# Routed feed-forward stage: results scattered to token order per tile in place of a gather at the end

## What is computed

```python
def _L3_ffn_ref(hidden_states, wg_red, wg, w1, b1, w2, b2):
    x = hidden_states.reshape(-1, c)
    xr = x @ wg_red.T
    wg_unit = wg / jnp.maximum(jnp.linalg.norm(wg, axis=1, keepdims=True), EPS)
    logits = xr @ wg_unit.T
    gates = jax.nn.softmax(logits, axis=1)
    indices_s = jnp.argmax(gates, axis=1)
    scores = jnp.max(gates, axis=1)
    for e in range(E):                      # E = 8 experts, hidden width 512
        mask = (indices_s == e).astype(x.dtype)[:, None]
        h = jax.nn.gelu(x @ w1[e] + b1[e], approximate=False)
        out = out + mask * (h @ w2[e] + b2[e])
    out = out * scores[:, None]
# and around it
g = _silu(_L3_ffn_ref(xn, ...))
x = x + s * g
```

## Time and profile before

| | |
|---|---|
| median of 3 runs | 6424.23 us (6416.99 to 6426.39) |
| profiled execution, its own time | 6420.27 us |
| its span, first to last instruction | 6418.5 us |
| PE busy | 5656.5 us, 88% |
| DVE busy | 4334.3 us, 68% |
| ACT busy | 3828.7 us, 60% |
| POOL busy | 2970.8 us, 46% |
| mean DMA rate | 35 GB/s |

### The profile page before, as it was taken

The page is one execution under the profiler, slowest core; times in us unless marked ns, Lnnn a source line. Parts: engine busy times, 40 slices in busy tenths (PEclk is TensorE's granted clock), DMA queues, the critical chain, the costliest instruction groups (busy, mean ns, idle before and its releaser), DMA issues. The chain is left out here.

```text
span 6418.5 us, 101900 instructions
## 1 busy us (share of the span) xinstructions
PE 5656.5 (88%) x33881; PEld 2996.4 (47%) x33881; DVE 4334.3 (68%) x9917; ACT 3828.7 (60%) x8010; POOL 2970.8 (46%) x2847
## 2 busy tenths in 40 slices
PE   8999998439999799999999889999999999896643
PEld 3444443312222466666666634444444444464443
DVE  4555553246666677777787678888888888685624
ACT  2444444126666577777777667777777777674322
POOL 1225234356777667666666433232332323154355
PEclk9999998769999899999999999999999999999876
DMA  1000001430000111111111110000000000031324
GB/s 38 8 11 30 14 17 34 122 81 11 14 13 8 54 33 32 30 33 39 40 46 44 35 29 12 19 10 12 19 12 19 10 12 17 17 89 44 107 68 122
DMA packets 348505, 225.99 MB, mean 35 GB/s; under 512 B 30290, under 2 KB 324946, under 8 KB 347730
## 3 DMA queue, kind: packets, MB, share of 16 engines
q1 hardware_dynamic: 328624, 183.83, 10.9%
q0 software_dynamic: 12288, 25.19, 1.5%
q10 hardware_dynamic: 7074, 10.46, 0.5%
HBM read 104.24 MB, written 68.55 MB: 27 GB/s over the span
## 5 line engine op out<-in xcount | busy, mean ns | idle before, releaser
L3816 PE MATMUL a_scores_ps<-a_kT,a_q_mixed 128*128 128x512 f32 x2048 | 1046.3, 593 | 3.7 <-ACT a_probs L3626 3.1
L3826 PE MATMUL a_acc_ps<-a_probsT,a_v_post 128*128 128x512 f32 x2048 | 1042.8, 592 | 0.4 <-DVE a_probsT L3719 0.4
L3626 ACT ACTIVATE a_probs<-a_scores_ps,a_neg_max 128x512 f32<-128x512 f32 x1024 | 703.0, 687 | 427.2 <-DVE a_neg_max L3709 417.9
L3709 DVE TENSOR_REDUCE a_neg_max<-a_scores_ps 128x1 f32<-128x512 f32 x1024 | 693.4, 677 | 202.4 <-PE a_scores_ps L3816 197.9
L3719 DVE STREAM_TRANSPOSE a_probsT<-a_probs 128x512 f32<-128x512 f32 x1024 | 715.4, 699 | 135.7 <-PE a_acc_ps L3826 112.2
L3631 ACT ACTIVATE a_probs<-a_probs,a_inv_sum 128x512 f32<-128x512 f32 x1024 | 727.8, 711 | 0.8 <-DVE a_inv_sum L3714 0.8
L2949 DVE TENSOR_REDUCE a_neg_max<-a_pair_ps 128x2 f32<-128x1024 f32 (+3 forms) x512 | 417.6, 824 | 353.8 <-PE a_pair_ps L3045 349.1
L2753 ACT ACTIVATE a_probsT<-a_pair_ps 128x1024 f32<-128x1024 f32 (+3 forms) x512 | 359.4, 704 | 483.8 <-PE a_pair_ps L3058 482.3
L3826 PEld LDWEIGHTS a_acc_ps<-a_probsT,a_v_post 128*128 128x128 f32 x2048 | 389.0, 190 | 490.9 <-issue 488.8
L3816 PEld LDWEIGHTS a_scores_ps<-a_kT,a_q_mixed 128*128 128x128 f32 x2048 | 384.4, 190 | 476.6 <-issue 438.9
L3572 POOL TENSOR_TENSOR a_q_mixed<-a_qT,a_pre 128x512 f32<-128x512 f32 x248 | 250.3, 1041 | 759.8 <-PE a_scores_ps L3816 759.8
(11 more groups left out here) (416 smaller groups left out, 11852.0 us busy)
## 6 DMA issues: line engine op xcount, KB each, us to landing
f_v_even<-f_v_odd SPq DMA_DIRECT2D x224, 130.0 KB, 2.3
attention_out<-a_s_out SPq DMA_DIRECT2D x64, 256.0 KB, 2.3
f_gs<-attention_out SPq DMA_DIRECT2D x64, 256.0 KB, 4.4
a_v<-a_v_rows SPq DMA_DIRECT2D x256, 64.0 KB, 2.1
a_x<-x_after SPq DMA_DIRECT2D x48, 256.0 KB
f_x<-x_after SPq DMA_DIRECT2D x48, 256.0 KB, 5.5
f_gx<-x_after SPq DMA_DIRECT2D x48, 256.0 KB, 3.3
x_after<-f_gout SPq DMA_DIRECT2D x32, 256.0 KB, 2.4
```

Source lines behind the costliest of these rows:

```text
L3626: act.activation(probs[:, n % NPR, :], scores_ps[n % NS][:], ACT.Exp, bias=neg_max[:, n % NS:n % NS + 1], scale=1.0, accum_out=row_sum[:, ...
L3709: dve.tensor_reduce(neg_max[:, n % NS:n % NS + 1], scores_ps[n % NS][:], AX.X, ALU.max, negate=True).then_inc(max_ready, 1)
L3816: pe.matmul(scores_ps[n % NS][:], q_mixed[:, g % 2, i].rearrange("f a q -> f (a q)"), kT[:, par, :], start=True, stop=True).then_inc(score ...
L3826: pe.matmul(acc_ps[par][:], v_post[:, g, i, :], probsT[:, g % NT, i, :], start=(p == 0), stop=(p == U - 1)).then_inc(products_done, 1)
```

## The change

The sorted rows get two more elements. Each row of x is now WIDE = 130 elements wide: 128 features, the number of the token (HOME) and its softmax weight (WEIGHT). The scatter carries both along, so a tile knows where its rows belong and how they are weighted. The rows of `x_sorted` are no longer filled with zeros from SBUF but with a constant array from DRAM, in which every row has a HOME of its own behind the last token, so that unused rows are scattered to a spare area.

In the tile loop, `add_b2` writes to a small buffer `y_tile` of two tiles. ACT multiplies by the weight into `y_tiles` (`weigh`, new), DVE converts the HOME column of each group to integers (`homes_of`, new), and POOL scatters each finished tile to `y_home` in DRAM (`scatter_tile`, new), eight tiles behind `pick_w1`. The gather at the end, DVE's weighting and the store to `y_sorted` are gone. After the last scatter has landed, SP loads the results of a batch from `y_home` with one plain DMA. POOL takes over s * y. The buffers of the finish are four deep where `gx` and `gs` were two deep, and `x_tiles` is six groups deep where it was four.

```diff
-        x = sb("x", [P, batches, NC, D])
+        x = sb("x", [P, batches, NC, WIDE])
-        y_tiles = sb("y_tiles", [P, 2, GROUP, D])
+        y_tile = sb("y_tile", [P, 2, D])
+        y_tiles = sb("y_tiles", [P, 4, GROUP, D])
...
         @block.sync
...
-                sp.dma_start(x_groups[g], zeros[:]).then_inc(zeroed, 16)
+                sp.dma_start(x_groups[g], fill_groups[g]).then_inc(filled, 16)
...
+            for n in range(4):
+                sp.wait_ge(y_scattered[n], 16 * GROUP * len(range(n, GROUPS, 4)))
+            for b in range(min(4, batches)):
+                load_y(b)
             for b in range(batches):
                 sp.wait_ge(out_ready, b + 1)
                 sp.dma_start(out_rows[b], out[:, b % 2]).then_inc(out_stored[b % 2], 16)
-                if b + 2 < batches:
-                    load_gate(b + 2)
+                if b + 4 < batches:
+                    load_y(b + 4)
+                    load_gate(b + 4)
...
         @block.gpsimd
...
+            def scatter_tile(i):
+                g, t = divmod(i, GROUP)
+                if t == 0:
+                    pool.wait_ge(homes_ready, g + 1)
+                pool.wait_ge(y_kept, i + 1)
+                pool.indirect_dma_start(y_home, bass.IndirectOffsetOnAxis(ap=homes[:, i:i + 1], axis=0),
+                                        y_tiles[:, g % 4, t, :], None).then_inc(y_scattered[g % 4], 16)
+            for i in range(TILES + 8):
+                if i < TILES:
+                    pick_w1(i)
+                if i >= 8:
+                    scatter_tile(i - 8)
...
-                    pool.indirect_dma_start(y[:, b % 4, c, :], None, y_sorted,
-                                            bass.IndirectOffsetOnAxis(ap=slot[:, n:n + 1], axis=0)
-                                            ).then_inc(gathered[b % 4], 16)
+                pool.tensor_tensor(gs[:, b % 4], gs[:, b % 4], y[:, b % 4], ALU.mult).then_inc(s_scaled, 1)
         @block.scalar
...
+            def weigh(i):
+                g, t = divmod(i, GROUP)
+                act.wait_ge(y_biased, i + 1)
+                if t == 0 and g >= 4:
+                    act.wait_ge(y_scattered[g % 4], 16 * GROUP * (g // 4))
+                act.activation(y_tiles[:, g % 4, t, :], y_tile[:, i % 2], ACT.Copy,
+                               scale=x_tiles[:, g % 6, t, WEIGHT:WEIGHT + 1]).then_inc(y_kept, 1)
-            for i in range(TILES + 1):
+            for i in range(TILES + 5):
                 if i < TILES:
                     keep_tile(i)
-                if i >= 1:
+                if 0 <= i - 1 < TILES:
                     gelu(i - 1)
+                if 0 <= i - 5:
+                    weigh(i - 5)
         @block.vector
...
+            dve.wait_ge(exp_ready, 1)
+            chain(dve.tensor_reduce(weight[:], diff[:], AX.X, ALU.add))
+            chain(dve.reciprocal(weight[:], weight[:]))
+            dve.tensor_copy(x[:, :, :, WEIGHT], weight[:].rearrange("p (b c) -> p b c", c=NC))
             dve.wait_ge(summed, 1)
...
                 dve.wait_ge(y_done, i + 1)
-                if t == 0 and g >= 2:
-                    dve.wait_ge(y_stored[g % 2], 16 * (g // 2))
-                dve.tensor_tensor(y_tiles[:, g % 2, t, :], y_ps[i % 2][:, 0:D], b2[:, bass.ds(e, D)],
-                                  ALU.add).then_inc(y_kept, 1)
+                if i >= 2:
+                    dve.wait_ge(y_kept, i - 1)
+                dve.tensor_tensor(y_tile[:, i % 2], y_ps[i % 2][:, 0:D], b2[:, bass.ds(e, D)],
+                                  ALU.add).then_inc(y_biased, 1)
+            def homes_of(g):
+                dve.wait_ge(tiles_loaded[g % 6], 16 * (g // 6 + 1))
+                dve.tensor_copy(homes[:, g * GROUP:(g + 1) * GROUP], x_tiles[:, g % 6, :, HOME]).then_inc(homes_ready, 1)
...
             def down(i):
...
-                    pe.wait_ge(y_kept, i - 1)
+                    pe.wait_ge(y_biased, i - 1)
```

More of the change, by code:

```diff
@@ L1437, in sorted_experts_phase @@
                  (rank[:], dram["L3f_rank"]), (below[:], dram["L3f_below"]), (steps[:], dram["L3f_steps"][:, 0:N]),
-                 (tile_no[:], dram["L3f_tile_no"][:, 0:TILES])]
+                 (tile_no[:], dram["L3f_tile_no"][:, 0:TILES]),
+                 (home[:], dram["L3f_home"][:, 0:N])]
         big_loads = [(w1[:], dram["L3f_w1"].rearrange("d n i -> d (n i)")),
@@ L1470, in _ @@
             sp.wait_ge(scattered, 16 * N)
-            for g in range(4):
+            for g in range(6):
                 load_group(g)
[L1473 to L1479, removed]
+            for b in range(min(4, batches)):
+                load_gate(b)
@@ L1480, in _ @@
+            for g in range(6, GROUPS):
+                load_group(g)
+            for n in range(4):
+                sp.wait_ge(y_scattered[n], 16 * GROUP * len(range(n, GROUPS, 4)))
+            for b in range(min(4, batches)):
+                load_y(b)
             for b in range(batches):
@@ L1506, in _, with pick_w1 @@
             pool.wait_ge(slots_ready, 2)
-            for i in range(TILES):
+            def pick_w1(i):
                 e = pool.value_load(at_i[0:1, i:i + 1], min_val=0, max_val=(E - 1) * I)
@@ L1606, in _ @@
             dve.wait_ge(weights, 16 * (len(loads) + 1))
+            dve.tensor_copy(x[:, :, :, HOME], home[:].rearrange("p (b c) -> p b c", c=NC))
             chain(dve.tensor_tensor(wg_sq[:], wg[:], wg[:], ALU.mult))
@@ L1696, in _ @@
                     add_b2(i - 2)
[L1698 to L1706 removed]
+                if i < TILES and i % GROUP == 2:
+                    homes_of(i // GROUP)
+            for b in range(batches):
+                dve.wait_ge(s_scaled, b + 1)
                 dve.wait_ge(sigmoid_ready, b + 1)
[L1708 removed]
+                chain(dve.tensor_tensor(gs[:, b % 4], gs[:, b % 4], gate[:, b % 2], ALU.mult))
                 if b >= 2:
                     dve.wait_ge(out_stored[b % 2], 16 * (b // 2))
[L1711 to L1717 removed]
+                dve.tensor_tensor(out[:, b % 2], gs[:, b % 4], gx[:, b % 4], ALU.add).then_inc(out_ready, 1)
         @block.tensor
@@ L3900, in constants @@
     out["L3f_tile_no"] = np.arange(NB * NC + 8, dtype=np.float32)[None, :]
+    out["L3f_home"] = (128.0 * np.arange(NB * NC)[None, :] + i).astype(np.float32)
+    fill = np.zeros(((NB * NC + 8) * P, D + 2), np.float32)
+    fill[:, D] = NB * T + np.arange((NB * NC + 8) * P)
+    out["L3f_fill"] = fill
     out["L1_window_mask"] = np.where(np.stack([seen & ((w == 1) | (same == 0)), seen], axis=1), 0.0,
```

98 lines of the change are left out of this document (42 added, 56 removed).

## The result

The changed kernel took **6442.4 us** (median of 8 runs, 6439.6 to 6453.7) against 6423.6 for the kernel before (8 runs, 6417.0 to 6426.4): ratio 1.0033, 95% interval 1.0022 to 1.0044. That is 18.8 us slower. Forecast were 6432 us and a range of 6416 to 6458. The profiled execution of after took 6442.71 us, its span 6441.0.

A forecast was written before the change was run, and what follows sets the result against it. Three parts in turn were taken as bound by POOL issuing indirect DMAs, PE, then POOL again. Loop +44.5, loop end +2.9, head +1.0 and last part -40.2 gave +8.2 on 6424.23: 6432 us, range 6416 to 6458.

The forecast's parts named there:

- a circle through `add_b1`, `gelu`, `weigh` and `add_b2`: Tile loop: with two places in `y_tile`, these instructions wait on each other in turn, setting a least 2.56 us a tile.
- The tile loop, forecast +44.5: Tiles 4 to 71: 2.56 us a tile against 1.896, over 67 tiles, 44.5 us added.
- `weigh` itself: a 128x128 ACT instruction took 0.26: Tile loop, on ACT: `weigh` priced at 0.26 us from an instruction that reads PSUM where `weigh` reads SBUF.
- The last part, forecast -40.2: After the tile loop: plain loads of y replace 64 gathers, 56.9 us against 97.1, 40.2 saved.
- the 3.6: End of the last part: 3.6 us from the end of the last DVE instruction to the end of the span.
- The end of the loop and the head: Five scatters behind the last `add_b1` add 2.9 us; the `home` load and earlier weight work before the slots add 1.0.
- The rival: Fill of `x_sorted` from DRAM comes late: at a third of 322 GB/s 3 us beyond cover, at a quarter 6450; chance 0.07.
- PE's pace: Tile loop: waits release earlier than read, so the 44.5 us fall away and the time is 6388; chance 0.13.
- The slower turn by register loads of 0.558: Tile loop: DVE's register load always at its longest, turn 2.82 us, loop 17.4 us longer, 6450; chance 0.13.
- The granted clock: Tile loop: PE's clock falls to the 1.2 GHz level, loop 63 us more, 6495; chance 0.05.
- the first case: Tile loop at 2.4 to 2.65 us a tile, end as forecast: own range 6418 to 6442, chance 0.62.
- three slow cases: Slower tile turns in the loop (0.13), a late fill (0.07) and a fallen PE clock (0.05).

## Why the prediction was right, and where it was off

- *Which way and how.* The forecast (a circle through `add_b1`, `gelu`, `weigh` and `add_b2` eats what the end saves) was right. It is shown from three sides: cutting it in either of two ways gives 1.894 us a tile, making a link shorter by 0.093 makes the period shorter by 0.093, and with the register load ahead the turn is again the sum of its links, 2.06.
- *The tile loop, forecast +44.5, measured +53.4.* This is the step that was off, and in it one term: "`weigh` itself: a 128x128 ACT instruction took 0.26" was 0.385. I had noted that it reads another source, and had left out that it has a scale from SBUF. 67 x 0.125 = 8.4 of the 8.9 us that are missing; three long turns (1.1 us) and a `homes_of` that costs its turn 0.03 and not 0.1 nearly cancel in the rest. The other four links were 0.73, 0.54, 0.20 and 0.82 against 0.73, 0.53, 0.20 and 0.81. The hand-over of 0.20 was a guess between 0.04 and 0.30 that no row had shown; that it came out is luck.
- *The last part, forecast -40.2, measured -38.7.* Errors cancel in part. The rounds took 3.23 us, not 3.6: reads and writes together ran at 325 GB/s, and from the first output to the end of the last DVE instruction it took 2.8 us less than forecast. But the first output was issued 7.8 us after the first load of y, not 5.6: DVE's first two products took 1.74 and 1.64 beside POOL's, and POOL's took 1.27, which the profile of before could not show. And 5.7 us, not 3.6, lay behind the last DVE instruction: the 3.6 were read from a program whose end did not wait for POOL, while now POOL's DRAIN ends last.
- *The end of the loop and the head.* +3.1 and +1.2 against +2.9 and +1.0. In the head `home` is about 0.9 us up to the logits and 0.4 at tile 4, so the +1.2 agree with the +1.0 only as a sum. The fill was hidden: the last of it was over by about 6087, 11 us before the scatter of x. The scatter's first DMA at 6098.0 is later than the 6094.5 that I had named as a sign of a late fill, but it waited for DVE's `slot`, and the whole phase had begun 3.5 us later. The rival had its edge at about a third of the zeros' 322 GB/s; alone the fill runs at 151, nearer to it than the 208 and 211 of all traffic in the stretches that it shares with loads of x and of the weights.
- *The rivals.* PE's pace could not be kept, since the circle is complete. The slower turn by register loads of 0.558 did not come: the median was 0.304 in 72. The granted clock did not fall, 1.00 in the loop with PE busy 81% (forecast 74%).
- *What the median hides.* The forecast was 10.4 us low, inside its range. By the stretches it is 8.9 for the loop, 1.5 for the last part and 0.4 for the two small ones, enough to move the result from what can't be told from no change to slower. The turn of 2.692 lies above the 2.4 to 2.65 of the first case, and the time 0.4 above its own range; what holds it is the room left for slow register loads or a late fill, and neither came, so that it lies inside the range is in part luck. Slower by more than 13 us had been given 0.38, less than the 0.47 for no change, and the parts named for it (three slow cases and a quarter of the first) add up to 0.41.

## What to carry to other kernels

When a stage is put behind another one with two buffers, write down for each wait what stands ahead of its releaser on that engine: a buffer wait becomes a circle if its releaser is queued behind work of the newest tile. The cure may be an order and not a buffer; here two swapped calls gave back 53 us. A register load in such a circle costs what hangs on its number too, and a link that is priced by a neighbour of the same shape needs the same operands.

## What was not expected of the hardware

- A register load on DVE takes 0.30 us, but with the two sequencer steps on its number it takes 0.52, and the next instruction stood idle for 0.53; issued one instruction earlier, it took 0.61 off the link.
- ACT, 128x128: 0.255 us from PSUM, 0.292 from SBUF, 0.385 from SBUF with a scale per row.
- At the end of the program POOL's DRAIN took 7.26 us from its last product on (6432.2 to 6439.5), and the program ended behind it, 1.8 us after SP had seen the last store land.
- POOL's product of two SBUF tiles, 128x512, took 1.27 us with DVE idle, where the one of the earlier trace rows, whose second operand is repeated along a row of 128, took 1.04. Whether that makes the difference was not tested.
- DRAM to DRAM in rows of 520 bytes went at 151 GB/s alone, with the DMAs at a share of 1.11.
- The start of the phase lay anywhere within 8.4 us (6021.2 to 6029.6) in fourteen traces, though the program ahead of it is the same. What moves it was not looked into.
